# An AdaLN mixture-of-experts layer: the experts' activation transposes placed inside the experts' unit

## What is computed

```
q_emb  = relu(cond @ W3 + b3)                        # one row per batch
h      = relu(((64*x + sum over the 64 tokens) * q_emb) @ W2 + b2)
scores = softmax(h @ gate_w.T)                       # 64 experts, the best 6 per token
for each expert e: buf[e] = up to 64 of its tokens   # CAP = 64
y[e]   = (silu(buf[e] @ w_gate[e]) * (buf[e] @ w_up[e])) @ w_down[e]     # 512 -> 352 -> 512
out    = x + sum over a token's slots of y * score + (silu(h @ sw_gate) * (h @ sw_up)) @ sw_down
```

## Time and profile before

| | |
|---|---|
| median of 3 runs | 1241.52 us (1240.71 to 1243.78) |
| the profiled execution, own time | 1234.47 us |
| its span, first to last instruction | 1232.7 us |
| PE busy over the span | 1217.3 us |
| DVE / ACT / POOL busy | 743.1 / 335.1 / 273.7 us |
| granted TensorE clock, mean | 0.999 of 2.4 GHz |

### The profile page before, as it was taken

One profiled execution on the slowest core, in us unless ns is written; L12 is line 12 of the kernel. 1 busy time (PEld: TensorE's weight loads), 2 busy tenths in 40 slices (PEclk: granted clock), 3 DMA queues, 4 the chain that ended last, 5 costly groups with the idle time before them and its releaser, 6 DMA issues.

```text
span 1232.7 us, 15783 instructions
## 1 busy us (share of the span) xinstructions
PE 1217.3 (99%) x5892; PEld 902.0 (73%) x5892; DVE 743.1 (60%) x1406; ACT 335.1 (27%) x631; POOL 273.7 (22%) x246
## 2 busy tenths in 40 slices
PE   7999999999999999999999999999999999999998
PEld 7877888888888888888766666666666666666666
DVE  7889998989889888886634333342333423423332
ACT  3555244433433443243211110110111201111111
POOL 0000000000000000000244255353443543535420
PEclk9999999999999999999999999999999999999999
DMA  8854437253543725246667988988989889899762
GB/s 182 225 137 139 111 99 182 73 154 90 146 109 89 188 73 152 58 138 204 245 225 238 324 285 248 351 275 272 320 253 310 301 282 296 286 278 320 264 144 78
DMA packets 159821, 250.91 MB, mean 204 GB/s; under 512 B 23616, under 2 KB 94400, under 8 KB 158592
## 3 DMA queue, kind: packets, MB, share of 16 engines
q1 hardware_dynamic: 143968, 223.66, 56.9%
q0 software_dynamic: 14048, 25.18, 10.0%
q10 hardware_dynamic: 1728, 1.05, 0.3%
HBM read 197.14 MB, written 61.10 MB: 209 GB/s over the span
## 4 chain that ended last, share of the span: by engine, by line
PE 95%; DVE 2%; ACT 1%; DMA 1%; issue 0%; SPq 0%; ACTq 0%
PE bank L1374 24%; PE bank L1376 23%; PE bank L1375 23%; PE bank L1568 12%; PE bank L1591 7%; PE bank L1420 1%; PE bank L1486 1%; PE bank L1423 1%; PE bank L1485 1%; PE bank L1577 1%; DMA x<-in_x_dram 1%; PE bank L1434 0%; DVE x L882 0%; DVE xpart L869 0%; DVE x L865 0%
## 5 line engine op out<-in xcount | busy, mean ns | idle before, releaser
L1374 PE MATMUL bank<-hh,gu 128*128 128x512 f32 x704 | 280.7, 399 | 0.8 <-ACT prod L691 0.8
L1376 PE MATMUL bank<-hh,gu 128*128 128x512 f32 x704 | 274.9, 390 | 0.0
L1375 PE MATMUL bank<-hl,gu 128*128 128x512 f32 x704 | 274.6, 390 | 0.0
L574 POOL DMA_INDIRECT hg<-table,idx_quarter x128 | 127.9, 999 | 642.7 <-DVE idx_hi L1263 604.0
L1374 PEld LDWEIGHTS bank<-hh,gu 128*128 128x128 f32 x704 | 132.3, 188 | 39.6 <-issue 14.0
L1376 PEld LDWEIGHTS bank<-hh,gu 128*128 128x128 f32 x704 | 132.2, 188 | 28.4
L1375 PEld LDWEIGHTS bank<-hl,gu 128*128 128x128 f32 x704 | 132.4, 188 | 25.6
L929 DVE TENSOR_TENSOR prod<-bank,prod 128x512 f32<-128x512 f32 x96 | 66.2, 689 | 129.4 <-PE bank L1376 113.9
L634 ACT ACTIVATE ah<-prod 128x512 fp32r<-128x512 f32 x96 | 60.7, 632 | 301.1 <-DVE prod L929 301.1
L1374 PE MATMUL bank<-sdh,ah 128*128 128x512 f32 x320 | 126.9, 397 | 0.0
L1376 PE MATMUL bank<-sdh,al 128*128 128x512 f32 x320 | 124.8, 390 | 0.0
(11 more groups left out here) (121 smaller groups left out, 1657.3 us busy)
## 6 DMA issues: line engine op xcount, KB each, us to landing
wg<-in_L_ffn_w_gate_dram SPq DMA_DIRECT2D x64, 704.0 KB, 9.1
wu<-in_L_ffn_w_up_dram SPq DMA_DIRECT2D x64, 704.0 KB, 10.6
wd<-in_L_ffn_w_down_dram SPq DMA_DIRECT2D x64, 512.0 KB, 5.3
table<-hrow SPq DMA_DIRECT2D x64, 256.0 KB, 4.3
x<-in_x_dram SPq DMA_DIRECT2D x60, 256.0 KB, 7.0
wd<-in_L_ffn_w_down_dram SPq DMA_DIRECT2D x64, 192.0 KB, 6.1
out_dram<-outst SPq DMA_DIRECT2D x36, 256.0 KB, 4.6
outst<-in_x_dram SPq DMA_DIRECT2D x32, 256.0 KB, 3.7
```

The costliest lines, as they stand in the source:

```text
L574: nc.gpsimd.indirect_dma_start(out=hg[p % 3][:, b, :], out_offset=None, in_=quarters, in_offset=bass.IndirectOffsetOnAxis(ap=idx_quarter[: ...
L1374: nc.tensor.matmul(o, st_h, mv_h, start=first_mm, stop=False)
L1375: nc.tensor.matmul(o, st_h, mv_l, start=False, stop=False)
L1376: return nc.tensor.matmul(o, st_l, mv_h, start=False, stop=last_mm)
```

## The change

In every unit the transposes of the pair before come first, then gate and up of this pair, then the down products of the pair before. The turns between the units are gone, but for one: the last pair's, half way before unit 32. DVE's work follows: `take_eactT(p - 1)`, `product_expert(p)`, `turn_rows(p + 1)`, `scale_y(p - 1)`. SP issues gate, up, down instead of down, gate, up.

```diff
@@ second_stage
-            done, p, turned = 0.0, 0, 0
+            done, p, turned = 0.0, 0, False
...
-                    elif turned < p and turned < NP and done >= FIRST_EXPERTS + (turned + 0.5) * EXPERTS_APART:
-                        yield "turn", turned, 0
-                        turned += 1
-            assert p == NP + 1 and turned == NP
+                    elif p == NP and not turned and done >= FIRST_EXPERTS + (NP - 0.5) * EXPERTS_APART:
+                        yield "turn", NP - 1, 0
+                        turned = True
+            assert p == NP + 1 and turned
@@ SP
-                if kind == "experts" and 0 < n < NP:
-                    load_down(n)
                 if kind == "experts" and n + 2 < NP:
                     load_gate(n + 2)
                     load_up(n + 2)
+                if kind == "experts" and 0 < n < NP:
+                    load_down(n)
@@ DVE
                 if kind == "experts":
-                    scale_y(n - 1)
+                    if 0 < n < NP:
+                        take_eactT(n - 1)
                     if n < NP:
                         product_expert(n)
+                        turn_rows(n + 1)
+                    scale_y(n - 1)
...
                 if kind == "turn":
                     take_eactT(n)
-                    turn_rows(n + 1)
@@ PE
             def experts(p):
+                if 0 < p < NP:
+                    actT(p - 1)
+                expert_gate_up(p)
                 expert_down(p - 1)
-                expert_gate_up(p)
```

## The result

| | before | after |
|---|---|---|
| median of 6 runs each | 1241.63 us (1240.71 to 1243.78) | 1254.45 us (1252.7 to 1258.95) |
| ratio, 95% interval | | 1.0103 [1.0092, 1.0115] |
| profiled execution, span | 1232.7 us | 1257.2 us |

The change makes the kernel 12.8 us slower. The forecast was +2.0 (1243.5), its range ended at 1250.0. The two profiled spans lie 24.5 us apart, not 12.8.

A forecast was written before the change was run, and what follows sets the result against it. PE's stream of work without holes was taken to bound the second stage; -0.5 (stream), +2.0 (copies) and +0.5 us (loads) gave +2.0, so 1241.5 became 1243.5 us, range 1239.5 to 1250.0.

The forecast's parts named there:

- PE's stream: Second stage on PE: moving transposes into units saves 0.02 us per unit, -0.5 us over the 31 turns that move.
- rival B's gain: PE's stream shortens more than accounted for: 1237 us, or 1231.7 if each turn's whole 0.38 us vanished; chance 0.09.
- The copies in units 2 and 15: Down products wait about 1.0 us in each unit for DVE's late copies of the transposes; +2.0 us together.
- `scale_y` last: DVE at the unit's end: free some 2.2 us behind it, before PE's next shared tile needs it; no wait.
- `turn_rows` early: DVE turns rows about 5 us earlier and can meet rows POOL hasn't brought; zero, up to 1 us at the upper end.
- The scatters' chain and the tail, zero: Down products end about 5.1 us later in a unit, but PE's last tile has 3.6 us of room; zero cost.
- The loads: Down weights, single-buffered, go last in SP's queue though wanted 5.07 us into the next unit; 0.5 us taken, 0 to 4.1.
- rival A: Down weights come late and PE's down products wait: 4.1 to 10 us, time put at 1247.5 us; chance 0.34.
- its six places: First down products of units 9, 10, 13, 14, 18 and 22, with margins of 0.5 to 1.3 us.
- With the third load landing as it does today nothing waits: Loads in SP's queue: no wait if landing is unchanged; 1.5 us of lateness would cost 4.1 us.
- The clock: A drop of PE's granted clock from 2.4 GHz at any of the waits; named, no cost given.
- no difference: Whole kernel: forecast together with case of copies' wait under 1 us and loads in time, 1241.5 +- 1; chance 0.57.

The follow-up runs named there:

- the run with closer units: The repaired kernel with EXPERTS_APART at 2.65 instead of 2.7; ratio 1.0028 [1.0014, 1.0041] to the kernel before.
- the repaired kernel: The changed kernel with SP's loads again down, gate, up and the four `split_h` moved to the next down tile; ratio 0.9995 [0.9986, 1.0004] to the kernel before.
- the other profile of the kernel before: The kernel before, unedited, profiled a second time on the chip where it takes 1233.2 us; 1233.11 us.
- larger pieces: The changed kernel with the first 256 rows of each expert's down weights read in 4 KB pieces, not 2 KB; ratio 1.0054 [1.0039, 1.0069] to the kernel before.
- the third profile: The changed kernel, unedited, run and profiled a third time; ratio 1.0083 [1.0069, 1.0098] to the kernel before.

## Why the prediction was wrong, point by point

- *PE's stream*: right. Forecast 0.02 us shorter a unit with 0.09 for transposes to gate; the trace has 0.09 for it and some 0.05 a unit. The cost of the switch stayed, in keeping with the rule of the Trainium skill that the prediction cites, and rival B's gain did not come.
- *The copies in units 2 and 15*: right in place and size. 2.0 us were forecast. Up to down took 3.37 and not 2.37 in unit 2 (the profile counts 1.6 to 1.7 us of idle PE for both); moving the splits away gave 2.5 us back.
- *`scale_y` last*: right, PE never waited for it. *`turn_rows` early*: right at this spacing in that no shared product of PE waited for it, but the bound of 1 us was too small for what it can do: 11.0 us of DVE and 2.6 of PE in the run with closer units.
- *The scatters' chain and the tail, zero*: right in most profiles; in one of the repaired kernel the 3.6 us of room were used up and 2.0 more.
- *The loads*: the mechanism was named (rival A), four of its six places too (units 9, 13, 18 and 22; units 10 and 14 never waited, and unit 5, which was not forecast, did in two profiles), and the size was wrong. **The step that failed is "With the third load landing as it does today nothing waits", and with it "I take 0.5 us" and the upper end of 1.5 us of lateness.** Two things were wrong in it. First the reading. The margins of 0.5 and 0.9 us for the loads of units 8 and 12 are those of the first of the up load's two DMAs; the landing of the second is missing from that trace. In the other profile of the kernel before the third load is complete 6.5 and 7.2 us into the next unit, and down is wanted 5.07 us in: landing as it does today it is 1.4 and 2.1 us late, and it is at these two places that the longest waits came. Second, I had argued that a full queue serves the same bytes by the same time in any order. It does not: full queues moved 261 to 410 GB/s, depending on what ran together, and the third load became 2 us later in the new order. The waits measured are 7.7 to 9.0 us where 0.5 stood in the sum. With the right landings and the 1.5 us the prediction's own sum would have been 4.1 - 1.0 - 0.6 + 2.9 + 3.6 = 9.0 us, an estimate. Writing an eighth of the output leaves 0.2 us of waits; larger pieces took perhaps a third. Why the loss is 8 us on one chip and 13 on another is open.
- *The clock*: named at the end as "something that I haven't costed at all". In unit 9 it made 2.80 us of down products 5.39. Over the three profiled executions of the changed kernel it added 1.6 to some 4 us to the waits.
- *What the sum would have been*: -1.5 for the stream (31 x 0.05), +2.0, +7.7 and +1.6 make 9.8 for the third profile; the median of its runs was 10.6 above before (1244.06 against 1233.47), the profiled execution itself 12.3 (1245.76). Of the 2.5 us that are missing there, 0.8 is a longer wait for the first transposed rows (1.3 us against 0.5); the rest has not been placed.
- *The likeliest case*: I gave 0.57 to no difference; rival A, at 0.34, came true. The waits of 7.7 to 9.0 us lie within its own price (4.1 to 10), but the upper end of the range had 6 us of waits, and nothing in it was for the slow clock.

## What to carry to other kernels

Order the loads of a loop by when each is wanted, and not by the order in which their buffers come free: the single-buffered weights that are wanted within one period belong ahead of the double-buffered ones, even if that holds the others back to the end of the unit. Read a load's landing from all of its DMAs: a row with "x2" and one single value to landing shows only one of them. And a margin against a load of 13 us on full queues is no margin where small packets of another queue run beside it. Behind a wait of some 3 us allow for slow clock: here it cost 1.6 to 2.6 us or nothing. And a transposition that is moved between its producer and its consumer needs the copying engine to be free at that moment: look for the one place where it has its longest batch.

## What was not expected of the hardware

Where the kernel before took 1241 to 1242 us, every profile taken beside it has PE nearly standing somewhere in 616 to 637 us, with nothing that the profile shows it waiting for: eight profiles, of eight different kernels. None of the eight profiles from the chips with 1233 us has it, nor has the one shown ahead of the prediction, whose execution took 1234.47 us. In the kernel before, PE ran 12 matmuls in 10 us at a granted clock of 0.61, as shown above, and its timeline reads:

```profile
626.26 0.58 PE L1374 MATMUL bank<-hh,gu 128*128 128x512 f32 x1 [1.55 <-issue]
628.37 0.58 PE L1375 MATMUL bank<-hl,gu 128*128 128x512 f32 x1 [1.53 <-issue]
```

ACT idled for 11.4 us in the same trace and began its silu of the first pair's gate only at 625.56. It is the time at which POOL issues its first indirect gathers; whether that is the cause was not tried.
